# Row gathers taken off SyncE's queue in a graph network: GpSimd makes all of them

## The reference

```
h   = relu(layernorm(x))                    # ahead of layer 0
msg = relu(h[src] + edge_attr)              # one row per edge
agg = segment_sum(msg, dst)
h   = relu(relu(batchnorm((h + agg) @ W1 + b1)) @ W2 + b2)
```

## Time and profile before

| | us |
|---|---|
| median of 3 runs | 3977.24 (3971.26 to 3994.51) |
| profiled execution, its own time | 4016.24 |
| its span in the profile | 4014.3 |
| POOL busy in the span | 1944.6 (48%) |
| PE busy | 2131.0 (53%) |
| DVE busy | 1694.4 (42%) |
| ACT busy | 732.8 (18%) |

### The profile page before, as it was taken

The page is one execution under the profiler, slowest core; times in us unless marked ns, Lnnn a source line. Parts: engine busy times, 40 slices in busy tenths (PEclk is TensorE's granted clock), DMA queues, the critical chain, the costliest instruction groups (busy, mean ns, idle before and its releaser), DMA issues.

```text
span 4014.3 us, 37448 instructions
## 1 busy us (share of the span) xinstructions
PE 2131.0 (53%) x9399; PEld 1315.4 (33%) x9399; DVE 1694.4 (42%) x2879; ACT 732.8 (18%) x1002; POOL 1944.6 (48%) x2048
## 2 busy tenths in 40 slices
PE   2454544444444454344434454353456887877878
PEld 1332323332232232222222232232233444444445
DVE  6554435445454443445445554444456111151112
ACT  3111112121111123122112222222234000020001
POOL 5555445455453523655554554455423455445552
PEclk8676666766666677666766776666767898888889
DMA  4222222222222232232332323333323444443442
GB/s 141 72 74 76 84 62 79 78 89 82 73 81 74 82 89 84 75 89 82 101 100 87 108 90 108 91 93 97 113 83 106 151 147 134 132 143 124 151 148 83
DMA packets 228500, 396.97 MB, mean 99 GB/s; under 512 B 43017, under 2 KB 132957, under 8 KB 228325
## 3 DMA queue, kind: packets, MB, share of 16 engines
q1 hardware_dynamic: 163300, 261.77, 19.8%
q0 software_dynamic: 65024, 133.30, 13.0%
HBM read 333.10 MB, written 61.81 MB: 98 GB/s over the span
## 4 chain that ended last, share of the span: by engine, by line
SPq 38%; issue 30%; PE 21%; another core or an unknown queue 6%; DVE 4%; ACT 1%; DMA 0%; DVEq 0%; ACTq 0%
SPq L524 28%; PE psA L1450 13%; SPq L520 6%; PE psG L1465 4%; SPq L503 1%; PE psG L1514 1%; SPq L499 1%; PE psG L1423 1%; SPq L538 1%; PE psA L1522 1%; DVE cell_room L1035 0%; DVE rows_h L902 0%; PE psA L1407 0%; PE psG L1544 0%
## 5 line engine op out<-in xcount | busy, mean ns | idle before, releaser
L629 POOL DMA_INDIRECT xg<-node_table,src_all x1520 | 1441.7, 948 | 1457.7 <-DVE xp_room L1048 891.0
L1407 PE MATMUL psA<-cell_room,xp_room 128*128 128x512 f16 (+1 forms) x2336 | 705.8, 452 | 1061.9 <-ACT count_out L696 621.0
L1423 PE MATMUL psG<-hid,xp_room 128*128 128x160 f32 x3072 | 582.5, 352 | 487.4 <-issue 278.9
L1035 DVE TENSOR_SCALAR cell_room<-psG,cell_all 128x932 f16<-128x932 int16 x1088 | 686.5, 690 | 199.9 <-remote 158.0
L1407 PEld LDWEIGHTS psA<-cell_room,xp_room 128*128 128x128 f16 x2336 | 258.9, 115 | 1492.2 <-issue 682.1
L1048 DVE TENSOR_TENSOR xp_room<-psG,xg 128x512 f32<-128x512 f32 x380 | 258.0, 679 | 1117.7 <-ACT psG L704 992.3
L649 POOL DMA_INDIRECT xg<-node_table,idx x480 | 469.0, 977 | 535.3 <-issue 380.2
L1423 PEld LDWEIGHTS psG<-hid,xp_room 128*128 128x128 f32 x3072 | 547.1, 233 | 520.1 <-issue 380.8
L704 ACT COPY psG<-xp_room 128x512 f32<-128x512 f32 x384 | 226.5, 590 | 1230.5 <-DMA xp_room<-in_edge_attr_dram 627.2
L696 ACT CAST count_out<-psA 128x1862 f16<-128x1862 f32 x96 | 164.2, 1710 | 1061.2 <-DMA count_store<-count_out 444.1
L1450 PE MATMUL psA<-cell_room,xp_room 128*128 128x456 f16 x1200 | 275.2, 383 | 99.6 <-issue 77.7
(11 more groups left out here) (154 smaller groups left out, 824.4 us busy)
## 6 DMA issues: line engine op xcount, KB each, us to landing
xp_room<-in_edge_attr_dram SPq DMA_DIRECT2D x98, 768.0 KB
cell_room<-count_store SPq DMA_DIRECT2D x16, 2850.0 KB
count_store<-count_out SPq DMA_DIRECT2D x96, 465.5 KB
hid<-count_store SPq DMA_DIRECT2D x16, 2736.0 KB
row_slot<-node_table SPq DMA_DIRECT2D x2048, 0.5 KB
xp_room<-in_edge_attr_dram SPq DMA_DIRECT2D x98, 256.0 KB
xg<-node_table,src_all POOLq DMA_INDIRECT x1520
node_table<-rows_h SPq DMA_DIRECT2D x48, 256.0 KB
```

The source lines that it names most:

```text
L629: nc.gpsimd.indirect_dma_start(xg[:, n % 2, u, j, :], None, x if n < RAW_TURNS else table, bass.IndirectOffsetOnAxis(ap=src_all[:, s, j:j ...
L1035: nc.vector.tensor_scalar(cells[:, c % CELL_RING, c0:c1], iota_bank[:, 0:c1 - c0], float(c0), cell_all[:, c:c + 1], ALU.add, ALU.is_equal) ...
L1407: last = nc.tensor.matmul(psA[:, bank, 0:w], src_hot[:, hots(n) % 2, at, :], cells[:, c % CELL_RING, c0:c0 + w], start=first, stop=end)
L1423: last = nc.tensor.matmul(psG[:, q, h * WIN:(h + 1) * WIN], ea[:, t, u, j, :], rows[:, u, j, :], start=(u == slots[0] and j == 0), stop=(u ...
```

## The change

The row gathers are removed. POOL's loop no longer leaves a slot out: it makes all 16 gathers in every turn, so 784 in each of layers 0 and 1. `slot_sum` always waits for POOL's gathers and always reads `xg`. SP's stream in layers 0 and 1 holds only loads and stores. `product`, which shared the memory of `row_slot` in layers 2 and 3, gets a tile of its own.

```diff
-ROW_SLOT = 2
-ROW_TURNS = (25, TURNS - 1)
-ROW_STARTS = (2, 26)
-ROW_STEP = 6
...
-        row_slot = sb("row_slot", [P, EPP * D])
-        product = row_slot[:, 0:UPG * CW].rearrange("p (s c) -> p s c", s=UPG)
+        product = sb("product", [P, UPG, CW])
...
-            def gather_rows(layer, t):
-                ...
-                    for p in range(p0, min(p0 + ROW_STEP, P)):
-                        _, rows = nc.values_load_multi_w_load_instructions(src_all[p:p + 1, s, :], ...)
-                        for j, row in enumerate(rows):
-                            sp.dma_start(row_slot[p:p + 1, j * D:(j + 1) * D],
-                                         table[bass.DynSlice(row, 1), :]).then_inc(row_landed[k], 16)
...
                         load_turn(n + RING)
-                    gather_rows(layer, n % TURNS)
...
                     for u in range(SLOTS):
-                        if by_rows(n, u):
-                            continue
                         h = u // len(HALVES[0])
-                        if n >= 2 and u == min(v for v in HALVES[h] if not by_rows(n, v)):
+                        if n >= 2 and u == HALVES[h][0]:
...
-                rows = xg[:, n % 2, u, :, :].rearrange("p j d -> p (j d)")
-                if by_rows(n, u):
-                    k, rows = ROW_TURNS.index(n % TURNS), row_slot[:, :]
-                    dve.wait_ge(row_landed[k], 16 * SUP * (n // TURNS + 1))
-                else:
-                    dve.wait_ge(gathered[n % 2][u], 16 * EPP * landed(n, u))
+                dve.wait_ge(gathered[n % 2][u], 16 * EPP * (n // 2 + 1))
```

More of the change, by code:

```diff
@@ L121, in units_in @@
     return [UNIT_OF[e] for c in chunks for e in (2 * c, 2 * c + 1) if e + 1 in UNIT_END]
[L124 to L131, removed]
 def parted(chunks):
@@ L379, in gnn_kernel @@
         gathered = [[sem(f"gathered{q}_{u}") for u in range(SLOTS)] for q in range(2)]
-        row_landed = [sem(f"row_landed{k}") for k in range(len(ROW_TURNS))]
         ea_staged = sem("ea_staged")
@@ L505, in load_turn @@
                              ).then_inc(ea_loaded[t], 16)
-            def gather_rows(layer, t):
-                for k, (first, used) in enumerate(zip(ROW_STARTS, ROW_TURNS)):
-                    p0 = (t - first) * ROW_STEP
-                    if not 0 <= p0 < P:
-                        continue
[L513 to L518, removed]
-                    for p in range(p0, min(p0 + ROW_STEP, P)):
-                        _, rows = nc.values_load_multi_w_load_instructions(
-                            src_all[p:p + 1, s, :], [mybir.EngineType.SP], min_val=0, max_val=NODES - 1,
-                            skip_runtime_bounds_check_because="the load checks its address against the table itself")
-                        for j, row in enumerate(rows):
-                            sp.dma_start(row_slot[p:p + 1, j * D:(j + 1) * D],
-                                         table[bass.DynSlice(row, 1), :]).then_inc(row_landed[k], 16)
             def store_table(version):
@@ L1041, in slot_sum @@
                 dve.wait_ge(ea_staged, (n - RAW_TURNS) * SLOTS + u + 1)
-                rows = xg[:, n % 2, u, :, :].rearrange("p j d -> p (j d)")
-                if by_rows(n, u):
-                    k, rows = ROW_TURNS.index(n % TURNS), row_slot[:, :]
-                    dve.wait_ge(row_landed[k], 16 * SUP * (n // TURNS + 1))
-                else:
-                    dve.wait_ge(gathered[n % 2][u], 16 * EPP * landed(n, u))
-                nc.vector.tensor_tensor(ea[:, n % RING, u, :, :].rearrange("p j d -> p (j d)"), ea_stage, rows,
+                dve.wait_ge(gathered[n % 2][u], 16 * EPP * (n // 2 + 1))
+                nc.vector.tensor_tensor(ea[:, n % RING, u, :, :].rearrange("p j d -> p (j d)"), ea_stage,
+                                        xg[:, n % 2, u, :, :].rearrange("p j d -> p (j d)"),
                                         ALU.add).then_inc(summed, 1)
```

## The result

In the job in which it was first timed, the changed kernel took 3654.88 us (median of 4, 3646.84 to 3664.60) against 3974.25 us for the kernel before (3965.82 to 3994.51) on the same chip: a ratio of 0.919, 95% interval 0.915 to 0.923, 319 us less. The profiled execution took 3655.34 us, 361 us less than that of before.

What follows compares the result with a forecast made beforehand. Row DMAs in SP's queue were taken to delay loads and stores in layers 0 and 1. 4016.24 - 400 + 10 = 3626 us profiled, less 39 us to the median: 3587, say 3590 us; range 3400 to 3740, widened to 3280 to 4000.

Steps and rivals of the forecast that it cites:

- What bounds the kernel: Layers 0 and 1: row DMAs in SP's queue delay loads and stores, making 88 turns 29.9 us on average.
- The turns after: Turns without row DMAs: 24.0 us in layer 0 and 26.7 us in layer 1, saving 264 and 136 us.
- The step to the runs' median: Profiled execution exceeds the runs' median by 39 us, taken as unaltered by the change: 3626 us becomes 3587 us.
- The upper end of the range: 3740 us, described as the lower bound of the saving (282 us) less the 20 us of gathers.
- The added gathers: POOL makes 16 more gathers at 1.26 us each: 0 to 20 us more, 10 taken.
- The second limit: PE nearly stands still during POOL's gather bursts, inferred to wait for instructions coming by DMA; the change leaves this in place.
- POOL becomes the bound: Rival: PE's slow stretches go with SP's row DMAs, turns fall to POOL's 20.1 us, 3135 us; chance 0.13.
- no change: Rival: POOL's bursts, not SP, set the turn; it stays 29.9 us, total 3977 to 3997 us; chance 0.13.
- Slower: Rival: bursts join up without POOL's pauses, turns reach 32.7 us, 246 us more, 4223 us; chance 0.14.
- Two rules that the prediction weighed: Skill rules set against its readings: PE starving for instructions, and SP's row DMA issue time of 13 to 41 us.

Runs made afterwards that it cites:

- e1: Changed kernel with SP again issuing the same 2048 row DMAs, into a buffer nobody reads; POOL still makes all gathers: 4031.88 us, 0.998 of the kernel before.
- e2: Kernel before with row gathers for turn 48 of each layer alone, turn 25 by POOL, so half the row DMAs: 3863.52 us, 0.953 of the kernel before.
- e3: Changed kernel without the gathers of slots 1 to 3 from turn 2 on in layers 0 and 1 (messages wrong): 2600.36 us, 0.642 of the kernel before.
- e6: Changed kernel with gathers of slots 1 to 3 from turn 2 on replaced by plain SP loads of as many bytes: 2579.04 us, 0.644 of the kernel before.
- e7: Changed kernel with 40 more semaphore increments on PE in every turn of layers 0 and 1: 3783.48 us, 0.9445 of the kernel before.
- e4: Changed kernel with one POOL wait a turn, for all four sums of turn n-2, in place of two: 3873.37 us, 0.956 of the kernel before.
- e8: e3 with 40 more semaphore increments on PE in every turn of layers 0 and 1: 2841.98 us, 0.7095 of the kernel before.
- e13: Kernel before, row DMAs kept, with POOL waiting for each slot instead of each half: 2764.08 us against 2763.52 us, ratio 1.0004.

## Why the prediction was right, and where not

- **What bounds the kernel (right, in an impeded job).** That the row DMAs made the difference is shown by e1, where they alone bring all of it back, and by e2, where it is paid in the turns that have them. That they did it by standing ahead of loads and stores is what SP's timeline shows.
- **The turns after (right, in part by luck).** Forecast 24.0 and 26.7 us, measured 24.5 and 26.6 us. The 24.0 us were the middle of two short row-free pieces, 21.3 and 26.7 us, for which no mechanism spoke. The measured turns saved 359 us for a forecast 400 us. The mis-sized term is layer 0's turn: 22 turns of 25.0 us and 22 of 24.2 us in place of 24.0 us give 237 for 264 us, and the two turns between, without rows before, became 3.6 us longer (23.2 us each for 21.3 us). In layer 1 the sum was made for 44 turns and 136 us; the 43 measured ones gave 126 us.
- **The step to the runs' median (off by 39 us).** I took the 39 us by which the profiled execution of before exceeded the median to be a property of the profile. That of the changed kernel was within 1 us of its own median, so it was none of the change; scatter between executions is the plain reading, and no run tests it. Of the 68 us between the sum's 3587 us and the measured 3655 us this is more than half, and the turns are the rest. The upper end of the range was 25 us too high by its own terms: 3977 - 282 + 20 is 3715 us, not 3740 us.
- **The added gathers (half a term, not seen in the impeded job).** 16 x 1.26 = 20 us, of which I took 10. In an impeded job e1 is no slower than the kernel before although POOL makes the 16 gathers as well. In free jobs the changed kernel is 12 us slower.
- **The second limit (its place right, its cause not).** That PE's slow stretches come with POOL's gathers and not with SP's row DMAs is shown by the changed kernel, which has them without any row DMA, and by e3 and e6, which have few gathers and no slow stretch; that the amount of traffic isn't the cause, by e6. That PE then waits for instructions which come by DMA is wrong: its instruction queue moved no packet while PE crawled and recovered. That its sequencer is slow, even on instructions that wait for nothing, is shown by e7. What the gathers take from the others' sequencers, and why only in some jobs, stays open.
- **The rivals.** A free job has the turn of "POOL becomes the bound", 20 us, but for both kernels and not as an effect of the change; and it has the number of "no change", 12 us for the gathers, but not its mechanism, since the turns aren't 29.9 us. That the forecast came true is luck in so far as the first job was an impeded one: nothing in a single profile of the kernel before could tell how common each kind is. "Slower" had a true core: longer bursts do cost, 4% in e4. But giving up the rows made bursts hardly longer (18.7 to 19.8 gathers).
- **Two rules that the prediction weighed.** By the Trainium skill, "Runtime: NRT & Kernel Launch", section "Instruction fetch mechanics", code streaming is mostly hidden. The traces agree: none moved in the slow stretch at the opening of layer 1 of either kernel, and my reading was wrong to doubt it. By the Trainium skill, "DMA: Bandwidth & Descriptors", section "Issuing engines are not separate DMA queues", starting DMAs on several engines saves only issue time, which is usually small. In free jobs this fits, since 13 us of issuing a turn cost nothing; in the impeded job SP's issue time was not small, and giving it up was worth 319 us.

## What to carry to other kernels

A small DMA costs its queue issue time (0.55 us here at best, up to 1.9 us on average over a batch of 24), and everything behind it in that queue waits: put latency-critical loads and stores where no batch of small DMAs stands ahead of them, and read the queue's own timeline, since no busy time shows it. It pays only where the queue, and not another engine, sets the turn: in free jobs it gained nothing. Measure a change of 10% in more than one job before it is believed: here the same pair of kernels gave 0.919 in one job and 1.005 in another. If engines stall beside GpSimd's gathers with no releaser named, shorten the bursts (a wait for each buffer slot in place of each half gave 2% in the changed kernel, and in a free job it cost the kernel before nothing).

## What the runs showed of the hardware

- The same program took 4044 us and 2764 us on the same chip, a quarter of an hour apart, with the runs of a job within 1.5% of each other. The gathers themselves took 948 ns in the impeded and 945 ns in the free execution of the changed kernel.
- In an impeded job PE issues a matmul every 2.8 us from about 11 us after the start of a burst of gathers until, in most cases, 2 to 5.5 us after its end (8 matmuls in 20 us); in a free one it runs 64 in 20 us beside gathers without a break. Semaphore increments on PE, which wait for nothing, take 0.7 us in such a stretch and 51 ns outside (e7, e8), and in the two slow stretches that open layer 1 no instruction packet moves.
- As many bytes loaded by plain DMAs from SP, always from the same 128 rows, leave the other engines alone: 148 GB/s with DVE busy for 97 of 100 us (e6).
- A row DMA of 512 bytes costs SP's queue 0.55 us undisturbed (e13), and in the impeded job 1.1 us on average over all 2048 and 1.7 us in the portion of the earlier trace rows.
